# A block with a slot FFN, attention and a second slot FFN: the first batches' fetch and normalisation moved into the setup, the slots' weights fetched during routing

## The reference

```python
x = x + 0.5 * _L0_ffn_ref(_layernorm(x, axis=-1), ...)
x = x + _L0_attn_ref(_layernorm(x, axis=-1), ...)
x = x + 0.5 * _L0_ffn_ref(_layernorm(x, axis=-1), ...)

# _L0_ffn_ref, cut
S = broadcast(slot_init)                                   # 64 slots x 256
ctx = concatenate([x, broadcast(S.mean(axis=1))], axis=-1)
h = gelu(ctx @ w1 + b1)                                    # 512 -> 128
route_logits = (h @ w2 + b2) / (abs(tau) + 0.1)            # 128 -> 64
topk_vals, topk_idx = top_k(route_logits, 8)
alpha = (one_hot(topk_idx, 64) * softmax(topk_vals)[..., None]).sum(axis=-2)
si = einsum('bts,btd->bsd', alpha, x) / (alpha.sum(axis=1) + 1e-08)[..., None]
gi, gh = si @ Wih.T + bih, S @ Whh.T + bhh                 # GRU cell -> S_new
... q, k, v of S_new by wq, wk, wv; attention over the slots; layer norm with ln_g, ln_b
out = einsum('bts,bsd->btd', alpha, y @ wvp + bvp) @ wo + bo
```

## Time and profile before

| what | us |
|---|---|
| median of 3 runs | 3435.56 (3433.14 to 3438.01) |
| the profiled execution | 3431.27 |
| its span in the trace | 3429.5 |
| setup, to the end of its last DVE instruction | 0 to 17.3 |
| first hidden matmul of the first FFN | 35.05 |
| first hidden matmul of the second FFN | 3122.03 |

### The profile page before, as it was taken

One profiled execution on the slowest core, in us unless ns is written; L12 is line 12 of the kernel. 1 busy time (PEld: TensorE's weight loads), 2 busy tenths in 40 slices (PEclk: granted clock), 3 DMA queues, 4 the chain that ended last, 5 costly groups with the idle time before them and its releaser, 6 DMA issues. The chain is left out here.

```text
span 3429.5 us, 61061 instructions
## 1 busy us (share of the span) xinstructions
PE 3255.2 (95%) x22618; PEld 1160.2 (34%) x22618; DVE 3007.2 (88%) x4484; ACT 2703.3 (79%) x5325; POOL 1069.0 (31%) x1021
## 2 busy tenths in 40 slices
PE   6998899999999999999999999999999999998997
PEld 4655222323232323232323232323232323224654
DVE  6866889999999999999999999999999998997865
ACT  5841588888888888888888888888888888887840
POOL 2440233333333232323232323232323232123410
PEclk8999799999999999999999999999999999999998
DMA  4336121313131313131313131313131312122336
GB/s 134 99 139 282 46 65 34 81 34 81 35 80 35 80 36 79 36 78 37 78 36 78 37 77 38 77 38 77 38 77 38 77 38 65 39 80 85 99 125 269
DMA packets 180619, 262.27 MB, mean 76 GB/s; under 512 B 92180, under 2 KB 132948, under 8 KB 165988
## 3 DMA queue, kind: packets, MB, share of 16 engines
q1 hardware_dynamic: 177700, 256.28, 26.9%
q10 hardware_dynamic: 2624, 2.10, 0.2%
HBM read 121.91 MB, written 51.38 MB: 51 GB/s over the span
## 5 line engine op out<-in xcount | busy, mean ns | idle before, releaser
L1706 DVE TENSOR_REDUCE attn_part_max<-attn_ps 128x2 f32<-128x1024 f32 x2048 | 2442.4, 1220 | 213.4 <-PE attn_ps L1839 178.2
L1959 ACT ACTIVATE attn_probs<-attn_ps 128x512 f32<-128x512 f32 x4096 | 2161.5, 598 | 366.6 <-PE attn_ps L1852 366.4
L1852 PE MATMUL attn_ps<-attn_q_rows,attn_k_rows 50*128 50x512 f16 x4096 | 1259.3, 384 | 43.2 <-ACT attn_probs L1959 25.2
L1839 PE MATMUL attn_ps<-attn_k_rows,attn_q_rows 48*128 48x512 f16 x4096 | 1130.5, 386 | 18.9 <-DVE attn_part_max L1706 18.2
L1852 PEld LDWEIGHTS attn_ps<-attn_q_rows,attn_k_rows 50*128 50x128 f16 x4096 | 308.0, 94 | 1329.6 <-ACT attn_probs L1959 1206.9
L1866 PE MATMUL attn_ps<-attn_probs,attn_v_even 128*32 128x512 f32 x4096 | 548.2, 607 | 0.0
L1866 PE MATMUL attn_ps<-attn_probs,attn_v_odd 128*32 128x512 f32 x4096 | 545.5, 605 | 0.7 <-ACT attn_probs L1959 0.7
L1596 POOL CAST attn_max_parts<-attn_max_whole 16x128 f16<-16x128 f32 x128 | 35.9, 280 | 1158.9 <-ACT attn_max_whole L1905 1158.8
L1839 PEld LDWEIGHTS attn_ps<-attn_k_rows,attn_q_rows 48*128 48x128 f16 x4096 | 224.3, 94 | 159.1 <-DVE attn_part_max L1706 138.6
L1800 PE MATMUL attn_ps<-attn_shared,attn_w_qk 128*128 128x256 f16 x1536 | 212.9, 276 | 1.3 <-PEq L26 1.3
L1641 POOL TENSOR_TENSOR attn_alpha_t<-attn_alpha_t 128x256 f32<-128x256 f32 x120 | 88.0, 733 | 294.5 <-ACT attn_alpha_t L1936 258.5
(11 more groups left out here) (216 smaller groups left out, 2741.4 us busy)
## 6 DMA issues: line engine op xcount, KB each, us to landing
attn_q_rows<-attn_alpha_t SPq DMA_DIRECT2D x384, 64.0 KB, 2.3
attn_k_rows<-attn_alpha_t SPq DMA_DIRECT2D x384, 64.0 KB, 2.3
ffn_x_back<-in_L_attn_x SPq DMA_DIRECT2D x16, 1024.0 KB, 13.2
after_first_ffn<-ffn_x_back SPq DMA_DIRECT2D x16, 1024.0 KB, 12.2
attn_slot_out<-attn_alpha_t SPq DMA_DIRECT2D x256, 64.0 KB, 2.3
attn_alpha_t<-inverse_denominators SPq DMA_DIRECT2D x32, 512.0 KB
attn_alpha_t<-after_first_ffn SPq DMA_DIRECT2D x16, 1024.0 KB, 9.9
after_attention<-attn_alpha_t SPq DMA_DIRECT2D x16, 1024.0 KB, 4.6
```

The source lines that it names most:

```text
L1706: dve.tensor_reduce(part_max[:, G % 2, j, :, t, half], pair, AX.X, ALU.max).then_inc(dve_emptied, 1)
L1839: last = pe.matmul(ps[:, bank + e, :], q_rows[rows_e, G % NG, j, t * P:(t + 1) * P], k_rows[rows_e, G % NG, j, half * HALF:(half + 1) * HA ...
L1852: pe.matmul(ps[:, bank, :], k_rows[rows_e, G % NG, h // 2, kt * P:(kt + 1) * P], q_rows[rows_e, G % NG, h // 2, half * HALF:(half + 1) * H ...
L1959: act.activation(probs[:, quad % NQ, h, :], bank_of(s, b0), ACT.Exp, scale=1.0 / (SCALE * SCALE)).then_inc(act_emptied, 1)
```

## The change

The setup gets x0, x1 and x2: SP fetches x0 first of all, x1 behind the slots, x2 behind w1. The six small arrays that SP had last go to ACT's queue in another order. The eleven arrays of the slot stage leave the setup; SP fetches them in the routing block behind x7. DVE takes the statistics of batches 0 and 1 in the setup and normalises all eight tiles of both; POOL takes their roots; PE turns batch 0 between the slots and the product with Whh; ACT takes over the six copies of Wih and Whh from DVE and takes batch 0's four groups. The routing block then begins with `AHEAD, TURNED = 2, 1`: statistics of batch 2 and hidden(0). In step 0 ACT's normalisation of batch 2 moves behind both pairs of row copies. The second FFN keeps its order; the attention's waits on the ahead semaphores count from the two batches and four groups of the setup.

```diff
 @block.sync   (setup)
+            load_x(0)
             sp.dma_start(wih[:, :, :], ...).then_inc(gates_loaded[0], 16)
             sp.dma_start(whh[:, :, :], ...).then_inc(gates_loaded[1], 16)
             sp.dma_start(slots[:, :], d["L0_ffn_slot_init"]).then_inc(slots_loaded, 16)
+            load_x(1)
             load(c.w1[:, :, :], ...)
             load(w1_mean[:, :, :], ...)
-            load(w2_raw ...); load(b2_raw ...); load(tau ...); load(b1 ...); load(c.gate_bias ...); load(hh_bias ...)
+            load_x(2)
 @block.scalar   (setup)
-            load(c.wq ...); ... load(c.bvp ...)
-            act.wait_ge(loaded_act, 16 * len(n_act))
+            load(c.gate_bias ...); load(hh_bias ...); load(b1 ...); load(tau ...); load(w2_raw ...); load(b2_raw ...)
+            for n, w_t in enumerate((c.wih_t, whh_t)):
+                flat = w_t[:, :, :].rearrange("p k g -> p (k g)")
+                for g in range(KT * MT * P // HALF):
+                    act.wait_ge(turned, 3 * n + g + 1)
+                    act.activation(flat[:, g * HALF:(g + 1) * HALF], ps[:, 3 * n + g, :], ACT.Identity).then_inc(copied, 1)
+            xn_flat = c.xn_t.rearrange("p k t -> p (k t)")
+            for f in range(FILLS):
+                act.wait_ge(c.ahead_turned, f + 1)
+                act.activation(xn_flat[:, f * HALF:(f + 1) * HALF], ps[:, 1 + f, :], ACT.Identity).then_inc(c.ahead_taken, 1)
 @block.gpsimd   (setup)
+            for i in range(c.PREPARED):
+                pool.wait_ge(c.ahead_var, i + 1)
+                pool.tensor_tensor(c.ahead_rstd[:, i, :], c.ahead_var_eps[:, i, :], c.neg_half[:, 0:TT], ALU.pow).then_inc(c.ahead_root, 1)
 @block.tensor   (setup)
             pe.wait_ge(copied, 2 * groups)
+            pe.wait_ge(c.ahead_normal, 1)
+            for f in range(FILLS):
+                for j in range(4):
+                    k, t = divmod(4 * f + j, TT)
+                    last = pe.transpose(ps[:, 1 + f, j * P:(j + 1) * P], c.x_first[0][:, t, k * P:(k + 1) * P], c.ident[:, :])
+                last.then_inc(c.ahead_turned, 1)
             pe.wait_ge(slots_taken, 1)
 @block.vector   (setup)
-            for n, w_t in enumerate((c.wih_t, whh_t)):
-                ...
+            statistics(0)
+            normalise(0)
             dve.wait_ge(turned, 2 * groups + 1)
             ...                                  # slots' copy, sum, mean
+            statistics(1)
+            dve.wait_ge(loaded, 16 * SMALL)
             ...                                  # tau, w2, b2, both_bias
+            normalise(1)
             dve.wait_ge(product_ready, 1)
             ...                                  # gh_t, hid_bias
 build_ffn, routing
-        AHEAD, TURNED = (3, 1) if ending else (0, 0)
+        LOADED, AHEAD, TURNED = 3, 3 if ending else c.PREPARED, 1
...
-                for b in range(AHEAD, B):
+                for b in range(LOADED, B):
...
+                    if not ending and b == R - 1:
+                        load_slot_weights()
...
-                if TURNED == 0:
-                    turn_rows(0, (0, 1, 2, 3))
...
-                if not ending:
-                    normalise(0)
-                    take_rows(0, (0, 1, 2, 3))
-                    normalise(1)
...
-                    if n % 2 == 0 and AHEAD <= n + 2 < B:
+                    if n % 2 == 0 and n > 0 and n + 2 < B:
                         normalise(n + 2)
                     if n + 1 < B:
                         take_rows(n + 1, (2, 3))
+                    if n == 0 and AHEAD <= n + 2:
+                        normalise(n + 2)
```

More of the change, by code:

```diff
@@ L155, in build_setup @@
         ps = own.enter_context(nc.psum_tensor("ps_setup", [P, 8, HALF], F32))
+        c.slot_weights_loaded = sem("slot_weights_loaded")
+        c.first_x_loaded = [sem(f"first_x_loaded{i}") for i in range(3)]
         gates_loaded = [sem("wih_loaded"), sem("whh_loaded")]
@@ L165, in build_setup @@
         slots_taken = sem("setup_slots_taken")
-        mean_ready = sem("slot_mean_ready")
         product_ready = sem("setup_product_ready")
         tau_step = sem("tau_step")
-        bias_step = sem("bias_step")
         block = own.enter_context(nc.Block())
-        n_sync, n_act = [], []
+        x = d["L0_attn_x"]
+        T = x.shape[1]
+        TT = T // P
+        FILLS = KT * T // HALF
+        c.PREPARED, c.PREPARED_FILLS = 2, FILLS
+        SMALL = 8
         @block.sync
@@ L242, in _ @@
             last.then_inc(product_ready, 1)
[L243 to L244 removed]
+            pe.wait_ge(slots_taken, 3)
+            pe.wait_ge(loaded, 16 * SMALL)
             for k in range(KT):
@@ L251, in _, with statistics, normalise @@
         def _(dve):
-            for n, w_t in enumerate((c.wih_t, whh_t)):
-                flat = w_t[:, :, :].rearrange("p k g -> p (k g)")
-                for g in range(groups):
-                    dve.wait_ge(turned, 3 * n + g + 1)
-                    dve.tensor_copy(flat[:, g * HALF:(g + 1) * HALF], ps[:, 3 * n + g, :]).then_inc(copied, 1)
+            def statistics(i):
+                dve.wait_ge(c.first_x_loaded[i], 16)
+                for t in range(TT):
+                    dve.bn_stats(c.ahead_stats[:, i, t, :], c.x_first[i][:, t, 0:D]).then_inc(c.ahead_step, 1)
+                dve.wait_ge(c.ahead_step, 2 * TT * i + TT)
+                dve.memset(c.waited[:, :], 0.0)
+                for t in range(TT):
+                    dve.bn_aggr(c.ahead_mean_var[:, i, t, :], c.ahead_stats[:, i, t, :]).then_inc(c.ahead_step, 1)
+                dve.wait_ge(c.ahead_step, 2 * TT * (i + 1))
+                dve.tensor_scalar(c.ahead_var_eps[:, i, :], c.ahead_mean_var[:, i, :, 1], EPS, None, ALU.add).then_inc(c.ahead_var, 1)
+            def normalise(i):
+                dve.wait_ge(c.ahead_root, i + 1)
+                for t in range(TT):
+                    last = dve.tensor_scalar(c.x_first[i][:, t, 0:D], c.x_first[i][:, t, 0:D], c.ahead_mean_var[:, i, t, 0:1],
+                                             c.ahead_rstd[:, i, t:t + 1], ALU.subtract, ALU.mult)
+                last.then_inc(c.ahead_normal, 1)
+            statistics(0)
+            normalise(0)
             dve.wait_ge(turned, 2 * groups + 1)
@@ L398, in _, with load_slot_weights @@
                     pack_last()
-                for b in range(AHEAD, B):
+                def load_slot_weights():
+                    wq, wk, wv, wvp, wo, bv, bq, bk, ln_g, ln_b, bvp = slot_weights
+                    for dst, src in ((c.wq, wq), (c.wk, wk), (c.wv, wv), (c.wvp, wvp), (c.wo, wo)):
+                        sp.dma_start(dst[:, :, :], src.rearrange("(k p) f -> p k f", p=P)).then_inc(c.slot_weights_loaded, 16)
+                    sp.dma_start(c.bv[:, :], bv.partition_broadcast(P)).then_inc(c.slot_weights_loaded, 16)
+                    for dst, src in ((c.bq, bq), (c.bk, bk)):
+                        sp.dma_start(dst[:, :], src.rearrange("(p o) -> p o", o=1)).then_inc(c.slot_weights_loaded, 16)
+                    for dst, src in ((c.ln_g, ln_g), (c.ln_b, ln_b), (c.bvp, bvp)):
+                        sp.dma_start(dst[:, :], src.rearrange("(m p o) -> p m o", p=P, o=1)).then_inc(c.slot_weights_loaded, 16)
+                for b in range(LOADED, B):
                     if b >= R:
@@ L404, in _ @@
                     sp.dma_start(x_slots[b % R][:, :, 0:D], rows(x_in, b)).then_inc(x_loaded[b % R], 16)
-                    if ending and b == AHEAD:
+                    if ending and b == LOADED:
                         spread_last()
@@ L408, in _ @@
                         store_last()
+                    if not ending and b == R - 1:
+                        load_slot_weights()
+                if not ending:
+                    sp.wait_ge(c.slot_weights_loaded, 16 * len(slot_weights))
             @block.gpsimd
@@ L468, in statistics @@
                     base = (b - AHEAD) * (2 * TT)
-                    dve.wait_ge(x_loaded[b % R], 16 * (b // R + (0 if b % R < AHEAD else 1)))
+                    if b < LOADED:
+                        dve.wait_ge(c.first_x_loaded[b], 16)
+                    else:
+                        dve.wait_ge(x_loaded[b % R], 16 * (b // R + (0 if b % R < LOADED else 1)))
                     for t in range(TT):
@@ L1992, in build_program @@
         weights = d["L0_attn_W_qkv"], d["L0_attn_b_qkv"], d["L0_attn_W_out"], d["L0_attn_b_out"]
-        build_ffn(nc, c, "ffn1", x, x1, d["L0_ffn_bo"], weights)
+        slot_weights = [d[f"L0_ffn_{n}"] for n in ("wq", "wk", "wv", "wvp", "wo", "bv", "bq", "bk", "ln_g", "ln_b", "bvp")]
+        build_ffn(nc, c, "ffn1", x, x1, d["L0_ffn_bo"], weights, slot_weights=slot_weights)
         nc.disable_value_cache = True
```

69 lines of the change are left out of this document (26 added, 43 removed).

## The result

The changed kernel takes 3424.91 us (median of 10 runs, 3422.61 to 3431.14), the kernel before 3434.70 beside it (10 runs, 3431.67 to 3438.01): 9.8 us less. The ratio of the means is 0.9974 (9.0 us) with a 95% interval of 0.9964 to 0.9983. The profiled execution of the changed kernel is one of its longer ones, 3428.66 us with a span of 3426.7, and that of the kernel before, 3431.27, is shorter than all of its ten runs; read against 3429.5 the changed span shows only 2.8 us, and where the rest of the 9.8 went in this execution has to be found in its rows.

The account below looks back on a forecast made before the run. The bound was taken as one serial chain before the first routing step, x being fetched only after the setup. Gains of 8.3 + 0.7 - 1.6 + 0 + 2.6 = 10.0 us gave 3425.6 us, range 3421 to 3432.

Parts of the forecast that it names:

- A: First FFN's routing: no slow spell in steps 1 to 3; 10.0 us gained, 3425.6 us; chance 0.40.
- B: First FFN's routing: the 1.2 GHz spell returns in one of steps 1 to 3; 7.4 us gained, 3428.2; chance 0.33.
- x0's landing: Setup: x0, first on SP's queue, lands at 7.5 us, 1.0 late from ACT's small loads; bounds 0 to 2 late.
- x1's landing: Setup: x1, behind 3.74 MB at 357 GB/s, lands at 15.1 us, in time by 1.4 us.
- VectorE's chain and the handover: Setup: VectorE's list ends at 26.0 us, handover 0.74, hidden(0) at 26.8 instead of 35.05; gain 8.3 us.
- hidden(0) at 1.2 GHz: Start of step 0: PE idle before it, so half clock costs 1.6 us, ends 0 and 2.6; step 0 gains 0.7.
- Step 1, ACT's late normalisation: Step 1, first FFN: normalising batch 2 ahead of Exp and Gelu makes the Gelu 1.6 us later; loss 1.6.
- Step 2: First FFN's routing: same order as before, ACT waits 2.05 us for POOL's shift; 12.44 us in both kernels, gain 0.
- What is gained is kept: After step 3: all later steps, slot stage, attention and second FFN are the same instructions, so the gain stays.
- C: Setup: loads slower, x0 at 8.5 and x1 at 18.5 us; sum 5 to 7 us, about 3429.8; chance 0.17.
- D: Handover: clock stays at 2.4 GHz, 1.6 us more, 11.6 gained, 3424.0 us; chance 0.07.
- E: Attention heads: a long 1.2 GHz stretch shifts into them, slower; must exceed 34 us to end above 3442; chance 0.03.

Follow-up runs that it names:

- e1: Changed kernel with ACT's normalisation of batch 2 in step 0 put back between the two pairs of row copies; 3426.53 us, ratio 0.9980 to before.
- e4: Changed kernel with the slots' eleven loads issued in the setup on ACT's queue again, not in the routing block; 3428.88 us, ratio 0.9990 to before.
- e6: Changed kernel with only batch 0 prepared in the setup, batch 1's statistics and normalisation back in the routing block; 3429.15 us, ratio 0.9981 to before.
- e8: e7 plus two groups of extra PE transposes in step 2 of the first FFN; 3427.11 us, ratio 0.9969 to before.
- e3: Changed kernel with batch 1's eight BN_STATS taken twice in the setup; 3427.18 us, ratio 0.9981 to before.
- e9: Changed kernel measured and profiled again, unaltered; 3426.87 us, ratio 0.9971 to before.
- e2: Changed kernel with 32 extra identity transposes at the end of PE's setup list; 3425.70 us, ratio 0.9979 to before.
- e7: Changed kernel with the edits of e1 and e2 together; 3429.06 us, ratio 0.9976 to before.
- e10: e8 with 42 instead of 32 extra transposes in the setup; 3426.74 us, ratio 0.9968 to before.
- e11: e10 plus extra transposes in the second FFN's routing and before the last batch's logits in both FFNs; 3423.51 us, ratio 0.9959 to before.

## Why the prediction was right, point by point

- **The result.** 3425.6 forecast, 3424.91 measured; faster by 0.26% (0.17 to 0.36), where over 0.2% was forecast. The likeliest case was A, though, no spell at 1.2 GHz in steps 1 to 3, and this is not what happened: the changed kernel has one in both of its profiles, as do e1 to e4 and e6. What came is rival B. By its own sum B would have gained 7.4 us; hidden(4) came 8.83 earlier in one profile and 8.32 in the other. So the mechanism was right (the chain of x0 and x1 fits into the setup), and that the median lies within 1 us of the forecast is partly luck: B's own sum gave 3428.2. From B's 7.4 to the 8.83 the terms go 0.3 for the earlier handover, 1.0 against it at hidden(0), 1.1 against it in step 1, 0.8 for it in step 2 and 2.5 for it in step 3. The medians and means gain 9.0 to 10.4 us, somewhat more than hidden(4) does; no run shows where the difference comes from.
- **x0's landing.** 7.5 taken, 6.83 measured, inside the 6.5 to 8.5 of the bounds. It landed 6.10 us after its issue against the 5.77 of the earlier trace rows, so the small loads beside it cost about 0.3 us, not 1.0. This 0.7 us gained nothing: VectorE lost it again waiting 0.77 us for the turned slots.
- **x1's landing.** 15.1 with 1.4 us to spare; in fact 16.4 (11.1 us after its issue), just as VectorE asked for it at 16.44. I had left out that SP's issue itself blocks: the slots' issue took 2.51 us and x1's went out at 5.29 only, and the stream fell to 227 GB/s between 8 and 10 us. The slack was not 1.4 but nothing (in e1 and e8 VectorE waited 0.17 and 0.38 us for x1), and e4 shows what lies behind it.
- **VectorE's chain and the handover.** Its end at 26.0, measured 25.68; hidden(0) at 26.8, measured 26.48. The terms (5.45, 2.76, 0.80, 1.31, 0.74) stood within 0.2 us. What the forecast left out is that x0 in front delays Wih from about 6 to 10.42 us and with it the turned slots to 15.7, just where VectorE's chain was forecast to need them: that 26.0 came out although x0 was early is chance. e3 shows that from the slots on the chain is the bound.
- **PE's cover.** Product at 22.4 by the sum, 20.75 in fact, asked for at 24.4: no wait, as said.
- **hidden(0) at 1.2 GHz.** Right that it would be, and mis-sized: 1.6 taken, 2.56 measured (6.26 against 3.70), and 2.97 in e9 (6.67), beyond the "at most 2.6". That bound was misread: hidden(3) of before, with its 6.18 us from 66.80, was not at 1.2 GHz to its end (the clock was back at about 71.7, see above). I had also moved the rise of the earlier trace rows, 3.7 us after PE began; here it came 5.2 us after, and 6.0 in e9.
- **Step 1, ACT's late normalisation.** 1.6 taken, 5.21 - 3.74 = 1.5 measured.
- **Step 2.** "12.44 in both" was wrong: 11.65. It took 11.65 to 11.67 us in the five profiles with the late normalisation and a spell in step 1 (changed, e9, e2, e3, e4), and 12.83 to 12.86 in the five with the normalisation back between the row copies (e1, e7, e8, e10, e11). No run separates the late place from the spell.
- **The spell.** It is where the case differs from both A and B: it fell in step 1 (45.3 to 52.1), not in step 3. There it made step 1 longer by 1.1 beyond the forecast's 10.1, and hidden(2) by 1.65, but that one ran beside ACT's normalisation and Exp and step 2 was not longer for it (11.65 to 11.67 us whether hidden(2) took 5.35 or 6.52). So it cost about 1.1 us where B had 2.6. Together: 8.57 + (10.79 - 11.08) + (8.52 - 11.23) + (12.44 - 11.65) + (13.01 - 10.54) = 8.83.
- **After hidden(4).** "What is gained is kept" holds for the work (137.0 to 137.1 us in all kernels but two, and before, changed and e9 have the same attention within 0.4 us), but single executions scatter by 5 us through spells in the second FFN, which the forecast had only as the spread of the three runs. e10 shows the limit of the argument: 4 us more in front, nothing in the median.
- **Rivals C, D, E.** C (late loads) did not occur, but x1 had no slack left. D did not occur. Nothing of E shows.

## What to carry to other kernels

Where a block ends in a chain and the next begins with one that needs only inputs, the second fits beside the first, if the engine that must do it has idle time: add up its list in order, for it becomes the new bound at once. Loads moved ahead displace others: count the bytes in front of each one on its queue and the issuing engine's own stalls; a companion edit that brings nothing alone (1.0002) was worth 3.3 us in the trace beside the first. And where PE waits in gaps of about two microseconds, a gain in front can be repaid later by a stretch at half clock, so compare medians of many runs, and use marks of the trace for steps below the scatter.
